# Issuing attention products in couples of neighbouring heads

## The reference

```python
x = x + layernorm(attn1(layernorm(x)))        # 16 heads of 16, rope, causal, context 250
x = x + layernorm(ffn(layernorm(x)))
# attn1: softmax(mask(q @ k.T * 16**-0.5)) @ v, then @ out_proj
# ffn:   s  = src + attn2(src) @ Wo           # 16 heads, rope, full 512 x 512, no mask
#        s  = rmsnorm(s)
#        out = swiglu(s @ W_shared_in) @ W_shared_out
#            + sum over the top 2 of 8 experts: gate_e * swiglu(s @ W1_shared) @ W2[e]
#        result = rmsnorm(s + out)
```

## Time and profile before

| | us |
|---|---|
| median of 3 runs | 2315.79 |
| lowest and highest | 2305.55, 2317.77 |
| the profiled execution, its own time | 2326.53 |
| its span, first to last instruction | 2324.5 |
| TensorE busy (share of the span) | 2059.2 (89%) |
| VectorE busy | 1385.1 (60%) |
| ScalarE busy | 831.0 (36%) |
| mean granted clock of TensorE | 0.881 |

### The profile page before, as it was taken

The page is one execution under the profiler, slowest core; times in us unless marked ns, Lnnn a source line. Parts: engine busy times, 40 slices in busy tenths (PEclk is TensorE's granted clock), DMA queues, the critical chain, the costliest instruction groups (busy, mean ns, idle before and its releaser), DMA issues.

```text
span 2324.5 us, 31756 instructions
## 1 busy us (share of the span) xinstructions
PE 2059.2 (89%) x9200; PEld 1081.4 (47%) x9200; DVE 1385.1 (60%) x4293; ACT 831.0 (36%) x1714; POOL 342.1 (15%) x647
## 2 busy tenths in 40 slices
PE   6868799898999989999898988989889999999986
PEld 4343445535364443635445353453635445354445
DVE  6456455755757465674667556476575745747454
ACT  2423424262433424334242532326233252423410
POOL 3322113101320003100031011210112001210000
PEclk7566889998998987989899898799899897889998
DMA  4003002010030101201021000211002110020212
GB/s 165 2 28 136 1 2 92 37 38 10 9 130 1 48 1 66 72 2 48 1 83 56 31 17 1 83 55 38 11 2 100 37 48 1 7 90 34 74 55 91
DMA packets 23089, 104.69 MB, mean 45 GB/s; under 512 B 3312, under 2 KB 14192, under 8 KB 18288
## 3 DMA queue, kind: packets, MB, share of 16 engines
q1 hardware_dynamic: 21168, 89.81, 10.7%
q0 software_dynamic: 1728, 12.58, 1.4%
HBM read 84.56 MB, written 16.78 MB: 44 GB/s over the span
## 4 chain that ended last, share of the span: by engine, by line
PE 68%; DVE 20%; issue 7%; ACT 3%; DMA 1%; DVEq 0%; POOL 0%; SPq 0%; POOLq 0%; ACTq 0%
PE fb L734 13%; PE fb L712 11%; PE sm L646 10%; PE ot L686 10%; PE st L672 5%; PE st L615 3%; DVE negmax L1013 2%; DVE acc L1201 2%; DVE stats L927 2%; PE st L631 2%; PE dn L615 2%; PE dn L654 2%; PE dn L698 2%; PE sm L672 2%; DVE sm L1010 1%
## 5 line engine op out<-in xcount | busy, mean ns | idle before, releaser
L536 ACT ACTIVATE probs<-st 128x512 f32<-128x512 f32 (+3 forms) x832 | 404.7, 506 | 486.1 <-PE st L672 438.6
L646 PE MATMUL sm<-k_t,q_t 48*128 48x512 f32 (+3 forms) x928 | 385.8, 496 | 102.6 <-DVE negmax L1010 49.3
L734 PE MATMUL fb<-w_r,h_r 128*128 128x512 f32 x1536 | 444.9, 426 | 13.2 <-DVE acc L1201 13.2
L1013 DVE TENSOR_REDUCE negmax<-sm 128x1 f32<-128x512 f32 x464 | 302.1, 686 | 136.2 <-PE sm L646 135.5
L646 PEld LDWEIGHTS sm<-k_t,q_t 48*128 48x128 f32 x928 | 170.8, 213 | 439.4 <-DVE negmax L1010 211.3
L672 PE MATMUL st<-q_t,k_t 64*128 64x512 f32 (+3 forms) x832 | 352.2, 478 | 14.3 <-ACT probs L536 12.1
L734 PEld LDWEIGHTS fb<-w_r,h_r 128*128 128x128 f32 x1536 | 279.8, 195 | 126.4 <-issue 60.1
L712 PE MATMUL fb<-xn_t,wup_s 128*128 128x512 f32 x512 | 321.5, 723 | 6.5 <-DVE h_s L1186 4.1
L1010 DVE CUSTOM_DVE_ANT_0 sm<-sm,mask_qk 128x384 f32<-128x384 f32 (+2 forms) x464 | 213.3, 467 | 190.9 <-PE sm L646 188.5
L686 PE MATMUL ot<-probs,v_s 128*32 128x512 f32 (+3 forms) x2048 | 276.3, 563 | 2.9 <-POOL probs L439 1.8
L672 PEld LDWEIGHTS st<-q_t,k_t 64*128 64x128 f32 x832 | 153.2, 203 | 135.1 <-ACT probs L536 87.1
(11 more groups left out here) (166 smaller groups left out, 2464.1 us busy)
## 6 DMA issues: line engine op xcount, KB each, us to landing
w_r<-w_parts SPq DMA_DIRECT2D x32, 2048.0 KB, 7.8
w_parts<-w_r POOLq DMA_DIRECT2D x4, 2048.0 KB, 8.9
x_s<-in_L_attn_query SPq DMA_DIRECT2D x8, 512.0 KB, 4.6
h_s<-in_L_ffn_W_experts POOLq DMA_DIRECT2D x8, 512.0 KB, 6.3
q_t<-rot_b SPq DMA_DIRECT2D x256, 4.0 KB
x_kept<-o_s SPq DMA_DIRECT2D x8, 512.0 KB, 3.0
xa<-x_kept SPq DMA_DIRECT2D x8, 512.0 KB, 3.5
out<-acc SPq DMA_DIRECT2D x8, 512.0 KB, 11.4
```

What stands on the lines that cost most here:

```text
L536: nc.scalar.activation(probs[:, n % PSLOTS, 0:hi - lo], score_bank(m)[:, 0:hi - lo], ACT.Exp, scale=float(D) ** -0.5).then_inc(s_ex, 1)
L646: mm(max_bank(w)[:, 0:hi - lo], q_t[r:r + MROW, b, t * P:(t + 1) * P], k_t[r:r + MROW, b, lo:hi], start=True, stop=True).then_inc(s_sm, 1)
L734: last = mm(fb[q % 2][:, :], h_r[:, h, m, rows], w2_r[:, k % 2, w, m, :], start=(m == 0 and n == 0), stop=(m == NH - 1 and n == 2))
L1013: return v.tensor_reduce(negmax[:, g % 2, n // GH, c:c + 1], max_bank(g * UNITS + n)[:, 0:hi - lo], AX.X, ALU.max, negate=True).then_inc(s ...
```

## The change

`LEAD_WIDE` becomes a pair of ranges, one per attention: 12 to 23 in the first, as before, and 0 to 23 in the second, so that maxima of the second attention use four banks from the first unit. And where four banks are open to a unit, it is issued together with the next: at an even step both units w and w + 1, at the odd step none. This holds for maxima of `LEAD_WIDE[a]` and for scores from unit 40. All the rest of a step (hidden and expert products, weighing, transposes) stays at its step. VectorE's, ScalarE's and GpSimd's queues have the same order as before.

```diff
-LEAD_WIDE, TAIL_WIDE = range(3 * GH, LEAD - GH), ALL - LEAD + 4
+LEAD_WIDE, TAIL_WIDE = (range(3 * GH, LEAD - GH), range(0, LEAD - GH)), ALL - LEAD + 4
...
-        def max_bank(u):
+        def max_bank(u, a):
 
-            return (sm + st)[u % 4] if u in LEAD_WIDE else sm[u % 2]
+            return (sm + st)[u % 4] if u in LEAD_WIDE[a] else sm[u % 2]
...
-                if w >= 2 and w - LEAD_WIDE.start not in (2, 3):
-                    back = 4 if w - 4 in LEAD_WIDE and w in LEAD_WIDE else 2
+                wide = LEAD_WIDE[a]
+                if w >= 2 and w - wide.start not in (2, 3):
+                    back = 4 if w - 4 in wide and w in wide else 2
                     pe.wait_ge(s_mx, i * N_MX + u - back + 1)
...
+            def in_pairs(w, wide):
+
+                return (() if w % 2 else (w, w + 1)) if wide else (w,)
+
             def attention(i, f, e, a):
...
-                    if m + LEAD < ALL:
-                        max_unit(i, a, *divmod(m + LEAD, UNITS))
+                    for w in in_pairs(m + LEAD, m + LEAD in LEAD_WIDE[a]):
+                        if w < ALL:
+                            max_unit(i, a, *divmod(w, UNITS))
                     if m >= 0:
...
-                        score_unit(i, a, g, n)
+                        for w in in_pairs(m, m >= TAIL_WIDE):
+                            score_unit(i, a, *divmod(w, UNITS))
```

More of the change, by code:

```diff
@@ L642, in max_unit @@
                 w = g * UNITS + n
-                if w >= 2 and w - LEAD_WIDE.start not in (2, 3):
-                    back = 4 if w - 4 in LEAD_WIDE and w in LEAD_WIDE else 2
+                wide = LEAD_WIDE[a]
+                if w >= 2 and w - wide.start not in (2, 3):
+                    back = 4 if w - 4 in wide and w in wide else 2
                     pe.wait_ge(s_mx, i * N_MX + u - back + 1)
-                mm(max_bank(w)[:, 0:hi - lo], q_t[r:r + MROW, b, t * P:(t + 1) * P], k_t[r:r + MROW, b, lo:hi],
+                mm(max_bank(w, a)[:, 0:hi - lo], q_t[r:r + MROW, b, t * P:(t + 1) * P], k_t[r:r + MROW, b, lo:hi],
                    start=True, stop=True).then_inc(s_sm, 1)
@@ L1008, in take_max @@
                     dve.sem_inc(s_seen[0], 1)
-                    scores = max_bank(g * UNITS + n)[:, 0:hi - lo]
+                    scores = max_bank(g * UNITS + n, a)[:, 0:hi - lo]
                     return v.tensor_tensor_reduce(scores, scores, mask_qk[:, BACK * P - (hi - lo):BACK * P], -1.0,
@@ L1013, in take_max @@
                 return v.tensor_reduce(negmax[:, g % 2, n // GH, c:c + 1],
-                                       max_bank(g * UNITS + n)[:, 0:hi - lo], AX.X,
+                                       max_bank(g * UNITS + n, a)[:, 0:hi - lo], AX.X,
                                        ALU.max, negate=True).then_inc(s_mx, 1)
```

## The result

| | before | changed |
|---|---|---|
| median (lowest to highest), us | 2316.78 (2305.55 to 2326.24), 4 runs | 2231.4 (2218.86 to 2237.8), 4 runs |
| profiled execution: span, us | 2324.5 | 2233.7 |
| its mean granted clock | 0.881 | 0.903 |
| TensorE busy, us | 2059.2 | 1971.4 |

The ratio is 0.9641 (95%: 0.96 to 0.9681). In what follows a *fall* is a place where the granted clock drops from 2.4 to 1.2 GHz for a while. A ratio leaves out runs that lie over 1.5% above a kernel's fastest, so for kernels whose runs spread widely it and the ratio of the medians differ.

A forecast was written before the change was run, and what follows sets the result against it. TensorE, busy 89% of the span, was taken as the bound; 19.2 + 2.4 + 14.7 + 7.2 + 3.2 + 3 = 49.7 us off the profiled 2326.5 gives 2277, as a median 2266; range 2243 to 2302.

The forecast's parts named there:

- those 26: Second attention, leads' end and middles, seven batches: the falling clock costs 26 us, of which 3 were taken as gain.
- First leads: First attention's leads, seven batches: pairing and a vanished wait save 2.1 us each, 14.7 in all.
- 0.58 wait: First lead, hidden product behind unit 16: its 0.58 us wait for VectorE's hidden step goes.
- First tails: First attention from unit 40: 12 slots for 17 save 0.9 us a batch, 7.2 over eight.
- Batch 0: Second lead of batch 0, without expert products: units 0 to 11 leave the two-bank pace, saving 2.4 us.
- Second leads: Second attention's leads, seven batches: four banks from unit 0 and fewer slots save 2.75 us each, 19.2 in all.
- the walk: Second attention, new order stepped through with traced durations: lead 22.5 us; tail +0.2 (units 40 to 47), -0.6 (48 to 63).
- Second tails: Second attention from unit 39: fewer slots against new waits save 0.4 us a batch, 3.2 in all.
- Unit 41's 0.7: Second tail: unit 41, issued right behind 39/40, needs exp 39, so TensorE is idle some 0.7 us.
- Rival 1: Both leads: VectorE takes over as bound and waits only move; 20 us gained, 2296; chance 0.20.
- Rival 4: Couples: bank waits hold each second product, so none share a slot; some 17 us gained, 2299; chance 0.05.
- Rival 2: First attention's tails: reshuffled timing brings more clock falls, 12.7 us each, up to 2332; chance 0.10.

The follow-up runs named there:

- e12: Changed kernel, with each maximum of the second attention taken over half of its columns: 2197.9 us.
- e7: Changed kernel, with units 24 and 25 waiting for the maximum four back instead of two: 2238.1 us.
- e5: Changed kernel, with heads reordered so both products of a couple use the same row half; number and place of instructions unchanged: 2329.3 us.
- e4: Kernel before, with couples of score products in both tails alone: 2313.3 us.
- e9: Changed kernel, with scores issued singly in both tails, couples kept in both leads: 2243.7 us.
- e3: Kernel before, with couples in the first lead alone: 2276.2 us.
- e13: Kernel before, with four banks from unit 0 in the second lead, no couples of maxima, and couples of scores in both tails: 2297.9 us.
- e1: Kernel before, with four banks from unit 0 for maxima of the second attention and no couples anywhere: 2280.9 us.
- e8: Changed kernel, with four banks and couples for maxima up to unit 27 in both leads and for scores from unit 36: 2202.2 us.

## Why the prediction was wrong

**The failed step** is the clock: "I take 3 us of those 26". Measured are about 21 us for the clock by the half-rate times of all runs, 25 by what the stages leave over, and most of them are not among "those 26", which were the falls at the second leads' end and in the middles behind. Of these, the leads gave 6 us (188.0 us for the seven before, 162.2 after, from first product to score 0, less the 19.6 of the stages), the middles 0.5. The rest came from stretches that the step did not price at all: in the profiled pair, half-rate time fell by 21 us in the middles and 23.5 in the tails of the first attention, by 16 and 13 behind the two tails, by 14 ahead of the first product for maxima and by 10 in the first leads. That pair is one execution of each kernel and differs by more than the medians do (120 us at half rate for 66), so it shows where such time can go and not each stretch's share. I had the first attention's tails, with 12.7 us a fall, only as a rival on the slow side. The half-rate time of one binary differs from run to run (425 to 553 us, with 2287 to 2327 us of time, over 55 runs of the kernel before), so a change of this kind was to be priced by that spread, to both sides, and not by one place in one trace.

The clock is not alone in it. Of the 36 us that the forecast of 50 lacks, 18 to 22 are the clock's and about 13 belong to terms that were undersized. Neither alone would have taken the time below the range: with the 47 us of stages as forecast and 21 of clock it is 2249, with 60 and 3 it is 2254.

**Undersized terms.** First leads, 14.7 forecast, 19.4 measured: I priced hidden products by their count and took 1.06 us each also where two became neighbours; they take 1.92 together, 0.2 less than twice that, for five such pairs a lead, and the hidden product behind the transposes of the maxima gains 0.2 in the same way. Of the 0.58 wait 0.44 remains. The new wait behind the gated half is 0.22 and not 0.35, but it also parts a pair, which then takes 2.40 us instead of 1.91. The slots themselves give 1.92: 1.92 + 5 x 0.20 + 0.20 + 0.14 - 0.49 = 2.77 us a lead, the 2.77 measured.

First tails, 7.2 forecast, 11.8 measured, 1.47 a tail. I counted 0.17 us for a score product that stood half covered behind a couple, and these four were priced too high: a threesome takes 0.43 or 0.36 us and the couple in its place 0.32 or 0.26, 0.44 us in all for 0.68. Unit 53, the one whole slot, gave 0.56 and not 0.37, since the transposes ahead of it and the hidden product behind it became neighbours, 0.2 again. And the group end, to which I gave a minus, gave 0.44: before, unit 48 took 0.59 us and the weighing behind it 0.89, of which 0.28 was a wait (921.29 to 922.76); now they take 0.38 and 0.66.

Batch 0: 2.4 forecast, 7.0 from first product to score 0 (25.0 and 18.0 us). Units 0 to 11 gave 3.5 of it, at half rate for most of the time, where I had priced the two-bank pace at full clock. Another 2.8 are behind unit 24, where before score 0 waited 2.05 us for the transfer of the placed maxima. That part isn't sure to be the change's: e12 has the same banks and couples, and there unit 24 to score 0 takes 5.8 us again.

**What held.** Second leads: 2.75 forecast, 2.8 measured, by the walk, with 22.4 us where it said 22.5, the wait of unit 11 gone and that of unit 25 left. Second tails: 3.2 forecast, 2.6 measured, with +0.22 us for units 40 to 47 and -0.58 behind them, where the walk said +0.2 and -0.6. Six couples that start together in the first lead. Unit 41's 0.7. Rival 1 (VectorE takes over, 20 us) is refuted as the case, though e7 shows that VectorE is the next bound: with unit 25 freed of its wait, units 26 and 27 wait. Rival 4 (no sharing) is refuted by the timelines; in e5, where it holds, nothing of the gain is left (1.0031), stages and clock together. Rival 2's mechanism is real: in e4 shorter tails are paid back by the clock, 546 us at half rate for 504. Why it did not decide in the change is not shown: from e9 to the whole the same tails come on top of couples in both leads, and half-rate time stays (439 and 437).

**Still open.** Why couples that run at once go with fewer falls at the entry of the second leads. From maximum 0 to 24, batches 1 to 7, profiled, the seven kernels with them from unit 0 on have 0 to 16 us at half rate, the eight without 0 to 85, and e5, whose couples don't share, 117. The two groups overlap (e3 has only 3.4 and before none), and each number is one execution. And why score couples without them raise half-rate time, by 42 us in e4 and by up to 66 in e13 (469 to 535, against e1; the kernel before had 503 in e1's group and 519 in e13's).

## What to carry to other kernels

Count mode changes of the matrix engine and not only instructions: a small product on half the rows cost 0.43 us alone, 0.33 each as two of one half, and 0.22 each as two at once, and a large product that stood beside another instead of beside a small one cost 0.2 less. Measure a stage up to work that the change does not move: up to score 63, which moved into a couple, the second tails seemed to win 0.8 us, and up to the product behind them it was 0.33. Price a change of TensorE's order with the granted clock of many runs of the kernel before, and give the clock term both signs: the same tails, 14 us shorter in their stages, were worth nothing by themselves and 12 to 15 us on top of couples in both leads. Once pairs are in, look for the next bound in the trace (here VectorE's maxima, behind which units 26 and 27 wait) and widen the pairs where banks are free, which gave another 25 to 29 us (e8), most of it in the second tails.

## What the runs showed of the hardware

- TensorE can be busy for all of a stretch and keep the 1.2 GHz level: 34.40 of 34.40 us in e5, at a clock of 0.53. The Trainium skill (TensorE: Matmul & The Clock Gate, Part 1) has the clock gate released by activity; the falls that vanish with VectorE's waits (e12) agree, this stretch, in which the engine never idled, does not. The same instructions at full clock, in the same kernel, take 21.00 us, and the profile does not show what tells the two apart.
- The time at half rate differs by a quarter of its median of 504 us between runs of one binary (425 to 553 us), and goes with most of their spread: 0.32 us of time for each.
- A change of TensorE between products on all rows and products on half of them costs about 0.2 us each way: a lone half-row product takes 0.43 us where the second of two adds 0.23 (e5), and two hidden products take 1.92 us together and 2 x 1.06 apart.
- Taking only the sharing away (e5) costs more by the clock than by the work: its second leads from maximum 0 to 24 take 21.0 us at full clock where the changed kernel's take 19.2, and its stages are some 36 us longer in all, yet it has 164 us more at half rate, worth 52.
